# One list of a megakernel reordered: transposes of x ahead of the last two gate/up groups, scaling of the heads behind the next turn's gate parts

## The reference

```python
x = x + tanh(g_xattn[0]) * mlstm(layernorm(x), ctx, ctx, Wi, bi, Wf, bf, ln_scale)
x = x + tanh(g_ffn[0]) * moe(layernorm(x), router_w, gate_w, up_w, down_w, shared...)

# mlstm, 16 heads of 64: gates from [q, k, v], a decay matrix D, scores times D
log_D = tril(cumsum(log_f)_s - cumsum(log_f)_t) + ig_t
D = exp(log_D - max_t log_D);  C = (q k^T / 8) * D
h = (C / (max(|sum C|, exp(-max)) + eps)) v;  h = layernorm_per_head(h) * ln_scale

# moe: 16 experts, the best two per token, and one shared expert for every token
shared = (silu(t @ shared_gate) * (t @ shared_up)) @ shared_down
routed = sum over the two chosen experts of w * (silu(t @ gate) * (t @ up)) @ down
```

## Time and profile before

| quantity | value |
|---|---|
| median of three timed runs | 2925.63 us |
| span of the profiled execution | 2941.0 us |
| PE busy | 2784.3 us, 95% of the span |
| DVE, ACT, POOL busy | 1845.4, 1015.8, 996.6 us |
| mix_block's merged turns, about 135 to 1049 us | 914 us, of which PE is busy 867.40 us |

### The profile page before, as it was taken

How to read it: one execution, slowest core, us unless ns; L and a number is a source line. 1 busy time by engine, 2 the same in 40 slices (tenths; PEclk the granted TensorE clock), 3 DMA queues, 4 the chain that set the end, 5 groups by cost and what they waited for, 6 DMA issues and landing times.

```text
span 2941.0 us, 49274 instructions
## 1 busy us (share of the span) xinstructions
PE 2784.3 (95%) x17322; PEld 2290.3 (78%) x17323; DVE 1845.4 (63%) x2800; ACT 1015.8 (35%) x1948; POOL 996.6 (34%) x1148
## 2 busy tenths in 40 slices
PE   3799999999999986999999999999999999999999
PEld 2677777777777774788888888888888888888887
DVE  3787878878887854454555545545545546767676
ACT  4445444444444421233333333333333331111111
POOL 1334433434344423343343443443443411111111
PEclk7799999999999997999999999999999999999999
DMA  6445545554555541344444444443443327666665
GB/s 196 148 158 170 159 141 162 166 153 152 162 169 159 145 166 65 136 150 150 145 150 148 146 153 144 146 153 143 148 152 143 100 108 213 182 203 183 203 182 182
DMA packets 243470, 458.24 MB, mean 156 GB/s; under 512 B 99696, under 2 KB 131824, under 8 KB 240624
## 3 DMA queue, kind: packets, MB, share of 16 engines
q1 hardware_dynamic: 116976, 333.62, 33.9%
q0 software_dynamic: 34880, 73.10, 8.1%
q10 hardware_dynamic: 91488, 49.82, 6.3%
HBM read 358.96 MB, written 115.31 MB: 161 GB/s over the span
## 4 chain that ended last, share of the span: by engine, by line
PE 59%; DVE 1%; issue 0%; ACT 0%; DMA 0%; SPq 0%; ACTq 0%; DVEq 0%
PE p_g_b L1608 19%; PE p_up_b L1608 19%; PE p_y_b L1594 19%; PE p_h_b L1581 1%; DVE x_t_b L1473 0%; DVE w_lo L1439 0%; DMA xn<-mid_xn 0%; ACT w_hi L1361 0%; SPq L1204 0%; DVE xt_lo_b L1479 0%; ACT xt_hi_b L1394 0%; DVE th_b L1485 0%; DVE x L1515 0%; DVE x L1506 0%; DVE y_b L1517 0%
## 5 line engine op out<-in xcount | busy, mean ns | idle before, releaser
L1300 POOL DMA_INDIRECT xn<-mid_xn,idx_q x284 | 304.5, 1072 | 512.6 <-DVE x_t_b L1473 424.6
L1608 PE MATMUL p_g_b<-w_hi,xt_hi_b 128*128 128x512 f32 x840 | 334.6, 398 | 19.8 <-DVE xt_lo_b L1479 16.9
L1594 PE MATMUL p_y_b<-w_hi,ht_hi_b 128*128 128x512 f32 x840 | 327.4, 390 | 1.9 <-DVE ht_lo_b L1462 1.9
L1608 PE MATMUL p_g_b<-w_lo,xt_hi_b 128*128 128x512 f32 x840 | 328.6, 391 | 0.0
L1608 PE MATMUL p_g_b<-w_hi,xt_lo_b 128*128 128x512 f32 x840 | 328.4, 391 | 0.0
L1608 PE MATMUL p_up_b<-w_hi,xt_lo_b 128*128 128x512 f32 x840 | 328.0, 390 | 0.0
L1608 PE MATMUL p_up_b<-w_hi,xt_hi_b 128*128 128x512 f32 x840 | 327.8, 390 | 0.0
L1608 PE MATMUL p_up_b<-w_lo,xt_hi_b 128*128 128x512 f32 x840 | 327.7, 390 | 0.0
L1594 PE MATMUL p_y_b<-w_hi,ht_lo_b 128*128 128x512 f32 x840 | 327.5, 390 | 0.0
L1594 PE MATMUL p_y_b<-w_lo,ht_hi_b 128*128 128x512 f32 x840 | 327.4, 390 | 0.0
L1462 DVE TENSOR_TENSOR ht_lo_b<-p_h_b,ht_hi_b 128x512 fp32r<-128x512 f32 x74 | 51.0, 690 | 367.5 <-ACT ht_hi_b L1377 367.5
(11 more groups left out here) (224 smaller groups left out, 5585.8 us busy)
## 6 DMA issues: line engine op xcount, KB each, us to landing
mid_y<-y_b SPq DMA_DIRECT2D x73, 512.0 KB, 2.6
stage<-mid_g_row SPq DMA_DIRECT2D x64, 512.0 KB, 5.4
stage<-in_eg SPq DMA_DIRECT2D x16, 2048.0 KB
stage<-in_eu SPq DMA_DIRECT2D x16, 2048.0 KB
stage<-in_ed SPq DMA_DIRECT2D x16, 2048.0 KB
mid_y<-in_x SPq DMA_DIRECT2D x34, 512.0 KB
stage<-in_x SPq DMA_DIRECT2D x32, 512.0 KB
stage<-in_ctx_t ACTq DMA_DIRECT2D x32, 512.0 KB, 8.9
```

The lines of the kernel that those rows point to most:

```text
L1300: nc.gpsimd.indirect_dma_start(out=xg_parts[:, n, :], out_offset=None, in_=xn_flat, in_offset=bass.IndirectOffsetOnAxis(ap=idx_q[:, n:n + ...
L1594: last = nc.tensor.matmul(p_y[n][:, :], a[:, k, :], b[:, GUP + k, w], start=(k == 0 and m == 0), stop=(k == FE // P - 1 and m == 2))
L1608: mm = nc.tensor.matmul(out[:, :], a[:, k, :], w[:, k, o:o + FE], start=(k == 0 and m == 0), stop=(k == KD - 1 and m == 2))
```

## The change

Three parts move in `TURN`. Q3 goes from the end of the list to a place ahead of K7 and K8. U1 goes to the end. D1 goes to the second place of the list, behind A2, and its offset becomes the -2 of `OFFSET`, since it now stands one turn later: it works on the same chunk as before. No instruction is added or taken away.

```diff
-        TURN = ("A2", "W1", "B0", "V1", "H1", "A3", "B2", "O1", "Y1", "E1", "P1", "A4", "E2", "A1", "B1", "W2", "Y2",
+        TURN = ("A2", "D1", "W1", "B0", "V1", "H1", "A3", "B2", "O1", "Y1", "E1", "P1", "A4", "E2", "A1", "B1", "W2", "Y2",
...
-                "E4", "W6", "Z1", "U1", "D1", "K7", "K8", "Q3")
+                "E4", "W6", "Z1", "Q3", "K7", "K8", "U1")
...
-        SHIFTED = {"U1": -2, "D1": -1, "K7": -2, "K8": -2}
+        SHIFTED = {"U1": -2, "K7": -2, "K8": -2}
```

## The result

The changed kernel takes 2939.08 us in the median of ten runs (2931.97 to 2946.71), the kernel before 2926.26 us on the same chip (2920.95 to 2930.56). The ratio is 1.0047, 95% interval 1.0036 to 1.0058: half a per cent slower. In a second measurement it was 1.0032 (1.0022 to 1.0043). The forecast was 2927.9 us and "the same". The kernel is slower by more than the forecast's own band allows (2921 to 2932); the time lies just inside the upper end of the wide range, 2940.

What follows compares the result with a forecast made beforehand. PE was taken as the bound, busy 867.40 of 914 us in the merged turns. The terms 8.7 - 11.1 - 7.2 + 11.9 = +2.3 us on the median of 2925.63 gave 2927.9 us; range 2921 to 2932, wide range 2913 to 2940.

Steps and rivals of the forecast that it cites:

- Part 1: Turn end on PE: A2's 22.8 us wait goes but returns at B2, 1.13 us a turn; +8.7 us net.
- Part 2, the late starts: D1 behind A2 ends late starts of `gparts` and `cmat` ahead of A3 and B2: -11.1 us, bounds 0 and -11.1.
- Part 2, A5's wait: POOL's product and E1 come sooner, near K + 6.1, so PE's wait ahead of A5 goes: -7.2 us.
- Part 3: Q3 on PE waits for ACT's copy of Q2, mostly in seven short turns: +11.9 us.
- Rival 1: Faster, 2918 us: Q2's copy comes earlier, so Q3's added wait costs 2 us instead of 11.9; chance 0.21.
- Rival 2: Slower, 2944 us: the wait for Q2's copy at Q3 becomes PE's bound, +18 over 28 turns; chance 0.14.
- Rival 3: Faster, 2903 us: all 22.8 us ahead of A2 go and nothing takes their place; chance 0.07.
- Rival 4: Slower, 2938 us: second scatters start inside D1's new window, POOL's product and E1 0.9 us later, 12.6 more; chance 0.12.
- Rival 5: Slower, 2950 us: granted clock falls after PE's idle times in seven short turns, +24 us; chance 0.04.

Runs made afterwards that it cites:

- small_d1: Changed kernel with DVE's product of D1 cut to one head of 16: ratio 0.9871 to the kernel before, merged turns 890.4 us.
- early_product: Changed kernel with Q2's copy ahead of F2, D1's two products exchanged and POOL's product ahead of its power: 2905.48 us, ratio 0.9918 to the kernel before.
- the four looks: Four more profiles of the unchanged kernel before: merged turns 906.4, 902.6, 903.9 and 901.3 us.
- before_again: The kernel before, unchanged, in a second profiled execution: ratio 0.9991, merged turns 906.4 us.
- before_look3: The kernel before, unchanged, in a third profiled execution: merged turns 902.6 us.
- d1_only: Kernel before with D1 moved behind A2 and Q3 left behind K7 and K8: ratio 1.0008 to the kernel before.
- q3_only: Kernel before with Q3 moved ahead of K7 and K8 and of U1, D1 left at its old place: ratio 1.0029 to the kernel before.
- q2_early: Changed kernel with ACT's copy of Q2 ahead of F2: ratio 0.9999 to the kernel before, merged turns 902.6 us.
- after_again: The changed kernel, unchanged, profiled and timed once more: ratio 1.0032 to the kernel before.
- late_scale: Changed kernel with Q2's copy ahead of F2 and D1's products exchanged, DVE's directly ahead of E1: ratio 1.0025 to the kernel before.
- before_look5: The kernel before, unchanged, in a fifth profiled execution: merged turns 901.3 us.

## Why the prediction was wrong

**Part 1, Q3 ahead of K7 and K8: right.** The 22.8 us ahead of A2 went and came back ahead of B2, from the DVE chain that was named; `small_d1` and `early_product` show it by taking D1 out of the chain. The size was too large: B2 and H1 idle 0.96 us a turn together instead of 1.13. Against the four looks, in the merged turns, L975 loses 22.8 us, L1044 gains 25.8 (26.0 less 0.2) and H1 0.8, so +3.8 and not +8.7.

**Part 2, the late starts: this step failed.** "I take all of this as gone: -11.1 us." After the change they were gone, but in four other profiles of before they are nearly absent too (L981 0.0 to 0.1, L1044 0.0 to 0.3 us in the merged turns), and the median did not contain them. In the merged turns that first profile is 7.5 to 12.6 us longer than the others, which is part of the 15.4 us by which its span stood above the median. I had seen that distance and carried the sum over to the median all the same, as if the two executions differed outside the merged turns. The cause given, D1 starting against the second scatter, falls as well: in `before_again` and `before_look3` second scatters start in the same window, 0.42 to 1.34 us after D1, in 9 and 14 turns, and `cmat` is on time. Without this term the sum is 2.3 + 11.1 = +13.4, and 2925.63 + 13.4 = 2939.0; 2939.08 was measured. That agreement is better than the terms deserve, since Part 1 was 5 us too large; that it meets the median is luck. What delayed `gparts` and `cmat` in that one execution stays open.

**Part 2, A5's wait: right.** Forecast -7.2, measured 7.2 to 1.7 against the first profile and 8.6 (the mean of four) to 1.7 against the others. E1 is at K + 6.02 to 6.04 in every turn. `d1_only` has 2.3 there and `q3_only` 0.1, so either half of the change takes the wait away, and not D1's place alone. What both have in common is that no first scatter starts inside D1 any more, as it does in the six turns of the earlier trace rows: in `q3_only` it starts by K + 0.68, ahead of D1, and in `d1_only` by K + 2.64, with D1 at K + 2.70. An early E1 in every turn is not needed: in `d1_only` it comes at K + 7.2 to 7.5 in 14 turns. On the median this gain doesn't show (1.0008).

**Part 3, the added wait: right.** Forecast +11.9, measured 9.9 and 10.8 in two profiles, 12 of them over the turns; the seven short turns have 8.1 us in both profiles (9.1 was forecast), the others the rest. `q2_early` takes it away and with it the whole loss.

**Put together** the seen terms are 3.8 - 6.9 + 10.4 = +7.3 us, near the 7.4 us that PE's idle time grew. PE's busy time grew by 2.4 us more, which the forecast had at nothing; where it comes from was not tried. The two make 9.8 of the 10.5 to 12.8 us between the medians.

**The rivals.** Rival 1 (the copy earlier) did not happen by itself; made to happen in `q2_early`, it gave 2929 (before beside it 2931) and not 2918, since its sum carried the same -11.1. Rival 2 (slower, the wait for the copy as PE's bound) has the right sign and place, but the wait is 10 us and not most turns'. Rival 3 (all of the 22.8 us, 2903 us) is what `early_product` comes near with 2905.5, by three more edits: Q2's copy early, D1's products exchanged, and POOL's product ahead of its power. Rival 4 did not happen in the changed kernel: the second scatters start at K + 1.5 to 2.1 (`after_again`: 0.5 to 2.1), all before D1. In `q2_early` it did: in 13 turns a scatter starts inside D1 and E1 comes at K + 6.8 or later, yet A5 waits only 3.5 us in all. What it would cost with Q2's copy at its old place was not seen. Its 2938 us is 12.6 above the median of before, while its text counts from the forecast, which would be 2940.5. Rival 5 did not happen in its size: the clock is 1.00 in all merged turns of the first profile after, and in `after_again` it fell for one stretch of 4 us behind the wait for Q2's copy, where the rival had seven. Even in the turn of the earlier trace rows, where the idle times ahead of H1 and B2 are the same 1.04 and 1.24 us, it stayed at full speed in both profiles after:

```profile
1050.94 0.66 PE L943 MATMUL p_tr<-ident,th 128*128 128x128 f32 x4 [1.04 <-DVE th L868]
...
1052.84 1.15 PE L1044 MATMUL p_u<-ctx_v,stage 128*64 128x65 f32 x32 [1.24 <-issue]
...
1053.00:1057.00 4.00, 4.00 (x62) 3.32 (x61) 3.29 (x5) 0.67 (x2) 1.46 (x1) 1.00 0.02 4
```

## What to carry to other kernels

When the span of the one profile lies above the timed median by more than the effect at stake, find the idle time in it that is irregular (late in some turns, with no release) and book none of it as won before a second profile shows it again; here four more did not. When a wait is taken from the bounding engine, list every chain that ends within a microsecond behind it; here there were three (the copy of Q2, D1 on DVE, POOL's product), and the move paid, 0.8% over the kernel before, when all were gone. A product of two factors can be split by when each factor is there: the one that needs nothing late goes to the idle engine early, the late one next to its reader.

## What the runs showed of the hardware

A small DVE instruction with two SBUF inputs is held until POOL's product is through, if that is running or starts with it. In `late_scale` `absf` took 0.28 us in the turns where the product ended by K + 4.25, and up to 2.49 us where it ended at K + 6.74. `cmat`, of the same queue and with one PSUM input, kept its 1.28 us. The Trainium skill, SBUF — State Buffer, section "SBUF: two separate sides", calls the shared pair of ports an exclusive lock, held for the whole instruction, for which a VectorE operation with two SBUF inputs and a GpSimd operation that reads SBUF compete, the one that starts first getting it. The trace agrees with the lock but not with the order: by the recorded starts `absf` was 0.13 us ahead of the product in the turn shown of `late_scale`, and 0.25 us in one turn of `q2_early`, and was held for 2.49 and 2.79 us all the same. Being held is not what cost `late_scale` its time, since D2 waits for the product itself.

POOL's scatters are held by D1 in turn. In the kernel before, in the turns where D1 runs from K + 2.04 to K + 3.26, the second scatters that start between K + 2.27 and K + 2.95 all end at K + 4.09, after 1.2 to 1.8 us instead of 0.96.

The pair of idle times of the earlier trace rows (1.04 and 1.24 us) was followed by a granted clock of 0.59 in the first profile of before, of 0.61 in `before_again` and of 0.52 in `before_look5`, each over 4 us, and by full speed in `before_look3` and in both profiles of the kernel after. A single wait of 1.98 us ahead of A5 was followed by 0.57 in `before_again` and by full speed in `before_look3`. No run here tells what decides it.
